# Expert weights laid out on the host in the order of the on-chip buffers: two transfers per pair of experts in place of four

## The reference

```python
def _L1_ffn_ref(hidden_states, router_weight, gate_up_proj, down_proj):
    # E = 64 experts, TOP_K = 8, CAPACITY = 256, H = 512, I = 192
    x = hidden_states.reshape(-1, H)
    probs = jax.nn.softmax(x @ router_weight.T, axis=-1)
    topw, topi = jax.lax.top_k(probs, K)
    topw = topw / jnp.sum(topw, axis=-1, keepdims=True)
    ...   # pos: each token's place in its expert's list; x_rep: x, K times over
    xe = jnp.zeros((E, C, H), x.dtype).at[flat_e, pos].set(x_rep, mode='drop')
    gu = jnp.einsum('ech,ehf->ecf', xe, gate_up_proj)
    g, u = jnp.split(gu, 2, axis=-1)
    ye = jnp.einsum('eci,eih->ech', jax.nn.silu(g) * u, down_proj)
    ...   # each token sums its K rows of ye, weighted by topw
```

## Time and profile before

| | |
|---|---|
| median of 3 runs | 5667.46 us (5666.89 to 5673.59) |
| the profiled execution: its own time | 5669.14 us |
| its span, first to last instruction | 5667.4 us |
| mean granted clock of PE | 0.919 |
| first layer of experts, SP's first weight load to POOL's last scatter | 2558.3 to 3324.0 us |
| second layer of experts, the same | 4880.0 to 5645.7 us |
| busy share of PE, DVE, ACT, POOL | 85%, 42%, 29%, 27% |
| q1's packets took, of 16 engines' span | 13.1% |
| q0's packets took | 12.3% |

### The profile page before, as it was taken

How to read it: one execution, slowest core, us unless ns; L and a number is a source line. 1 busy time by engine, 2 the same in 40 slices (tenths; PEclk the granted TensorE clock), 3 DMA queues, 4 the chain that set the end, 5 groups by cost and what they waited for, 6 DMA issues and landing times. The chain is left out here.

```text
span 5667.4 us, 66951 instructions
## 1 busy us (share of the span) xinstructions
PE 4820.4 (85%) x26288; PEld 2581.4 (46%) x26288; DVE 2362.7 (42%) x3233; ACT 1644.4 (29%) x2764; POOL 1527.4 (27%) x951
## 2 busy tenths in 40 slices
PE   6045988789999999985999949999999989589996
PEld 2013433333333333244655626666666654465654
DVE  1754588537666666744211122333333320512111
ACT  2511555120455555732111112222222210211111
POOL 0011000100577777011444430111111110044444
PEclk9567999899999999986999979999999999699998
DMA  1000000000000000013888840000000021368887
GB/s 46 0 9 17 16 0 0 0 32 1 1 1 1 1 1 1 1 55 112 221 224 226 226 87 25 29 23 29 31 29 31 21 101 61 131 172 224 218 225 164
DMA packets 223978, 395.83 MB, mean 70 GB/s; under 512 B 30480, under 2 KB 118544, under 8 KB 223632
## 3 DMA queue, kind: packets, MB, share of 16 engines
q1 hardware_dynamic: 166352, 249.13, 13.1%
q0 software_dynamic: 57344, 142.64, 12.3%
HBM read 288.88 MB, written 107.02 MB: 70 GB/s over the span
## 5 line engine op out<-in xcount | busy, mean ns | idle before, releaser
L2163 PE MATMUL linb_pr_ps<-lin_z,linb_wt 128*128 128x512 f32 x1536 | 677.8, 595 | 16.4 <-POOL linb_slope_own L2133 16.4
L1365 ACT ACTIVATE attc_prob<-attc_ps 128x512 f32<-128x512 f32 x1024 | 549.1, 596 | 443.0 <-PE attc_ps L1276 442.2
L1239 POOL TENSOR_TENSOR attc_acc<-attc_acc,attc_prob 128x2048 f32<-128x2048 f32 x120 | 547.9, 4566 | 121.6 <-ACT attc_prob L1365 109.2
L1389 DVE TENSOR_REDUCE attc_peak<-attc_ps 128x2 f32<-128x1024 f32 x384 | 469.6, 1225 | 258.0 <-PE attc_ps L1284 258.0
L1276 PE MATMUL attc_ps<-att_q,att_k 32*128 32x512 f32 x2048 | 528.6, 616 | 0.0
L1284 PE MATMUL attc_ps<-att_k,att_q 32*128 32x512 f32 x1536 | 450.0, 663 | 0.0
L2163 PEld LDWEIGHTS linb_pr_ps<-lin_z,linb_wt 128*128 128x128 f32 x1536 | 286.1, 191 | 342.1 <-issue 324.8
L2339 DVE SCALAR_TENSOR_TENSOR linb_gated<-linb_osb,linb_norm_w,linb_proj 128x512 f32<-128x512 f32 x64 | 94.4, 1474 | 668.1 <-ACT linb_osb L2266 668.1
L2140 POOL TENSOR_TENSOR linb_sq<-linb_osb 128x512 f32<-128x512 f32 x64 | 70.1, 1095 | 1039.0 <-ACT linb_osb L2266 1039.0
L1297 PE MATMUL attc_ps<-attc_prob,att_v 128*32 128x256 f32 (+1 forms) x3472 | 316.5, 437 | 0.3 <-ACT attc_prob L1365 0.3
L886 DVE TENSOR_TENSOR_SCAN ssmb_state<-ssmb_decay,ssmb_bu 128x2048 f32<-128x2048 f32 x64 | 279.7, 4409 | 78.9 <-ACT ssmb_decay L833 78.9
(11 more groups left out here) (510 smaller groups left out, 7652.8 us busy)
## 6 DMA issues: line engine op xcount, KB each, us to landing
moe1w_wgu<-in_L_ffn_gate_up_proj SPq DMA_DIRECT2D x32, 1536.0 KB
moe2w_wgu<-in_L_ffn_gate_up_proj SPq DMA_DIRECT2D x32, 1536.0 KB
moe1w_wd<-in_L_ffn_down_proj SPq DMA_DIRECT2D x32, 512.0 KB
gated_features<-linb_gated SPq DMA_DIRECT2D x64, 256.0 KB
moe2w_wd<-in_L_ffn_down_proj SPq DMA_DIRECT2D x32, 512.0 KB
linc_gt<-gated_features SPq DMA_DIRECT2D x7, 2048.0 KB
linb_wt<-in_L_attn_b_qkv_w SPq DMA_DIRECT2D x16, 768.0 KB
residual_rows<-residual SPq DMA_DIRECT2D x2, 4096.0 KB
```

The costliest lines, as they stand in the source:

```text
L1239: pool.tensor_tensor(acc[:, n % 2, :, :], before, prob[:, U % NP, :, :], ALU.add).then_inc(pool_done, 2 if at == 1 else 1)
L1365: nc.scalar.activation(prob[:, U % NP, h, :], ps[:, n % 3 if at < 0 else at % 6, :], ACT.Exp).then_inc(exp_done, 1)
L1389: V.tensor_reduce(peak[:, w // TT % 2, i % QH, 2 * hp:2 * hp + 2, b], ps[:, bank:bank + 2, :], axis=AX.X, op=ALU.max).then_inc(mx_used, 1)
L2163: last = nc.tensor.matmul(pr_ps[:, use % 2, :], wt[:, b, kind, k, :], z[:, k, t * NB:(t + 1) * NB], start=(k == 0), stop=(k == DT - 1))
```

## The change

The host reorders two inputs before the launch. `gate_up_proj` becomes (pair, partition, expert of the pair, k, column), so that what one partition of `wgu` takes is one stretch of 3072 numbers (12288 B) in DRAM; before, it was eight rows of 384 numbers (1536 B) in eight places. `down_proj` becomes (pair, partition, three rows of 512): the row of the first expert, that of the second, and the tail row, one stretch of 6144 B; before, it was three rows of 2048 B. `wd` and `wd_tail` become one buffer `wd` with three rows per partition, so each pair has two transfers in place of four. The bytes are the same, and PE reads the same numbers in the same order.

```diff
-        wd = W.sb("wd", [P, PW, 2, D])
-        wd_tail = W.sb("wd_tail", [P, PW, D])
+        wd = W.sb("wd", [P, PW, 3, D])
...
-        wgu_dram = g.dram["L1_ffn_gate_up_proj"].rearrange("e (k p) f -> p e k f", p=P)
-        wd_dram = g.dram["L1_ffn_down_proj"].rearrange("e p d -> p e d")
+        wgu_dram = g.dram["L1_ffn_gate_up_proj"]
+        wd_dram = g.dram["L1_ffn_down_proj"]
 
         def load_pair(sp, j):
             r = j % PW
-            sp.dma_start(wgu[:, r, :, :, :], wgu_dram[:, 2 * j:2 * j + 2, :, :]).then_inc(w_loaded[r], 16)
-            sp.dma_start(wd[:, r, :, :], wd_dram[0:P, 2 * j:2 * j + 2, :]).then_inc(w_loaded[r], 16)
-            for x in range(2):
-                sp.dma_start(wd_tail[x * TAIL:(x + 1) * TAIL, r, :], wd_dram[P:IN, 2 * j + x, :]).then_inc(w_loaded[r], 16)
+            sp.dma_start(wgu[:, r, :, :, :], wgu_dram[j, :, :, :, :]).then_inc(w_loaded[r], 16)
+            sp.dma_start(wd[:, r, :, :], wd_dram[j, :, :, :]).then_inc(w_loaded[r], 16)
...
-        W_LOADS = 4 * 16
+        W_LOADS = 2 * 16
...
-                        nc.tensor.matmul(ye_ps[:, y % 3, :], h[rows, j % 2, 2, cols], wd_tail[rows, j % PW, :],
+                        nc.tensor.matmul(ye_ps[:, y % 3, :], h[rows, j % 2, 2, cols], wd[rows, j % PW, 2, :],
...
+def expert_rows(a):
+    pairs = a.reshape(E_N // 2, 2, IN, D)
+    whole = pairs[:, :, 0:P, :].transpose(0, 2, 1, 3)
+    tails = pairs[:, :, P:IN, :].reshape(E_N // 2, P, 1, D)
+    import numpy as _np
+    return _np.concatenate([whole, tails], axis=2)
...
+    "L1_ffn_gate_up_proj": lambda a: a.reshape(E_N // 2, 2, DT, P, 2 * IN).transpose(0, 3, 1, 2, 4),
+    "L1_ffn_down_proj": lambda a: expert_rows(a),
```

More of the change, by code:

```diff
@@ L1490, in moe @@
             moe_routing(nc, g, name + "b", logits, index)
-        moe_experts(nc, g, name + "c", index, wgu, wd, wd_tail, w_loaded, load_pair, last)
+        moe_experts(nc, g, name + "c", index, wgu, wd, w_loaded, load_pair, last)
 def moe_logits(nc, g, name, logits, load_pair):
@@ L1802, in _, with moe_experts @@
                 lanes(q)
-def moe_experts(nc, g, name, index, wgu, wd, wd_tail, w_loaded, load_pair, last):
+def moe_experts(nc, g, name, index, wgu, wd, w_loaded, load_pair, last):
     with Layer(nc, name) as L:
```

## The result

| | before | after |
|---|---|---|
| device time, median of 4 runs | 5669.05 us (5666.89 to 5673.59) | 5716.23 us (5707.56 to 5728.7) |
| ratio to before | | 1.0088, 95% interval 1.0071 to 1.0105 |
| the profiled execution: its own time, its span | 5669.14, 5667.4 us | 5707.56, 5705.9 us |
| 28 rounds, first and second layer | 576.9, 577.5 us | 616.4, 618.4 us |
| DVE's wait at the two barriers | 12.6, 12.4 us | 0.8, 0.8 us |

The account below looks back on a forecast made before the run. It took the expert rounds to be bound by POOL's wait for scatters A to land, lengthened by weight loads. 5669.1 - 22 (barriers) + 62 (rounds) = 5709, less 1.7 to the median: 5707 us; range over all cases 5603 to 5772.

Parts of the forecast that it names:

- the two terms: Whole kernel: fewer starts at the two barriers give back 22 us; longer rows in 56 rounds cost 62 us.
- The barriers, -22 us: Barriers behind the router blocks: eight starts no longer held, saving 11.1 us in the first layer and 11.0 in the second.
- The rival that counts bytes: Router-block barriers: SP is held by bytes, so barriers stay and rounds grow, 5731 us; chance 0.07.
- The rounds, +1.1 us each, +62 us: Expert rounds: long rows ahead of scatters A lengthen each of 56 rounds, range +0.3 to +1.9 us.
- The price of the rows: Loads on q1: 472 ns per 12288 B row and 245 ns per 6144 B row, 5.74 us a load.
- all of it passes ahead of A, none is left for the gaps beside A: Rounds, q1: a load's 16 rows per engine fit within q0's 20 turns, so a round pays up to 5.74 us.
- the rival of equal bytes: Rounds: queues take turns of equal bytes, so each round is 0.7 us shorter, 5607 us; chance 0.30.
- A wait of 9.4 us in every round: POOL in the rounds: the wait between scatters A and B grows to near 9.4 us, a round to 21.7.
- Its test by the wait between A and B alone: POOL in the rounds: the forecast's sign is wrong if that wait is under 8.3 us.
- Whole rows: Loads on q1: long rows travel uncut, about 288 packets for a load in place of 1472.
- The rival of cut rows: Loads on q1: 12288 B stretches travel in pieces as short as now, rounds stay, 5647 to 5669 us; chance 0.05.
- At most 1.24 us a round to gain: Rounds: PE becomes the bound once its 1.24 us wait for gathered tiles is gone, 69 us in all.

Follow-up runs that it names:

- late_long: Changed kernel, long rows throughout, but SP starts a pair's load only after POOL has started scatters A four pairs earlier; 5744.28 us, ratio 1.0125.
- after_a_long: Changed kernel, all rows long, but SP starts a pair's load only when POOL has seen scatters A land; 5595.9 us, ratio 0.986.
- after_a_short: Against first_four (same rows): SP starts a pair's load only when POOL has seen scatters A land; 5571.57 us, ratio 0.9822 to the kernel before.
- the down-only kernels: Loads started just behind scatters A's start, only down weights loaded inside rounds (work left out); short rows 5559.5 us, long 5560.77, against the kernel before 0.9791 and 0.9794.
- first_four: Against the changed kernel: long rows only for pairs 0 to 3, short rows in four transfers for pairs 4 to 31; 5649.61 us, ratio 0.9956 to before.

## Why the prediction was right, and where it was not

The sign, the time (5707 against 5716) and the two terms came out. That the time is so close is in part luck: the two terms measure +57 us in place of the +40 of the forecast, and the medians show +47, with a router block whose clock differs between executions. Point by point:

- *The barriers, -22 us.* Measured -23.4. That what fills up is counted in rows is shown by the series: 88, 56 and 24 rows of equal bytes, DVE's wait 9 to 13, 5.6 to 5.7 and about 1 us. The rival that counts bytes is out.
- *The rounds, +1.1 us each, +62 us.* Measured +1.44, +80 us: within the +0.3 to +1.9 given, and mis-sized by taking the middle. The price of the rows was also low: by the DMA view of the first layer's rounds q1 took 28.8% of 616.4 us, 6.3 us a load and not 5.74. The full 5.74 us is what `late_long` pays, 10.05 and 10.27 behind A less the 4.43 of the earlier trace rows, 5.6 to 5.8, but as a late start and slower packets and not as a load ahead of A.
- *"all of it passes ahead of A, none is left for the gaps beside A".* This step failed. In the changed kernel 65 load packets still stood beside 64 of q0 late in A, and q1 was not empty before A's last packets. The prediction counted packets ahead of A, 20 turns against 16 rows, and took the turns to begin with the load. (Of the 36 packets per engine that it counted on q0, 5 to 6 carry 4 B each and 15 are of the gathers.) In fact 3 to 4 us of a load hold A back, with short rows and with long ones, and the rest runs beside A. Before, that rest was nearly free: of the 3.9 us paid, 5.43 - 2.33 = 3.1 are the late first packet and 4.80 - 4.39 = 0.4 the slower packets. With long rows beside it A takes turns with rows of 245 ns to 0.840 x 3.0 x 16 / 82 = 0.49 us: 10 of them lengthen A by 6.86 - 4.39 = 2.5 us, where 25 to 34 short ones cost 0.4 to 0.8. (The price of one long row is not constant: 0.25 us here, 0.28 in the changed kernel, but 0.11 for B of `after_a_long`.) That turns go by packet was right; so the rival of equal bytes is out: beside 0.40 MB of q1 it would have put as much of q0, and 0.13 was there. The rule cited from the Trainium skill (DMA: Bandwidth & Descriptors, section Queues, rings and completion order) agrees with the 65 to 64, where a turn of the load is one row.
- *A wait of 9.4 us in every round.* The mean was 8.63 and 8.97, most rounds 8 to 11 us, and about one in five 4 to 6. The prediction took every load to meet A and forgot that the next A waits for B. In one round of five the load meets B, whose landing then comes 9.2 to 12.2 us behind its start. In such a round A misses the load and waits little; the loss stands ahead of A. Its test by the wait between A and B alone, wrong in sign if under 8.3 us, can mislead, since only the sum of both idle times shows the loss: with tiles gathered four pairs ahead that wait was 7.8 us and the kernel still slower than before. That PE's wait for tiles grows (66.3 for 34.8 us) was foreseen; A does not wait for PE.
- *Whole rows.* The packets of the execution fell from 223,978 to 148,201, by 1184 for each of 64 loads: 1472 - 1184 = 288 each, as forecast. The rival of cut rows is out.
- *At most 1.24 us a round to gain.* Too low: in `after_a_short` the round gained 1.22 us and PE still waited 0.64 us for tiles, and the down-only kernels gained 1.4 to 1.7. PE's busy time was taken as fixed, but at a granted clock of 1.00 in place of 0.96 it fell from 542 to 525 us a layer.

## What to carry to other kernels

In this kernel long rows on one queue were cheap for themselves and dear for the short rows of a neighbour that something waits for, because the queues took turns by packet. So lengthen rows where a queue is filled ahead of a barrier, and test it with care beside scatters or gathers that something waits for. When a transfer lengthens another's wait, first move its start to where other work covers the wait: that gave 78 us with short rows here (`first_four` to `after_a_short`; 76 by the ratios) and 120 with long ones (the changed kernel to `after_a_long`; 129 by the ratios), while the rows' length decides 24 us between the two ends. Judge a wait in a loop together with the idle time ahead of it: a load that misses one pair of scatters may meet the next, and then the loss stands in another place.

## What the runs showed of the hardware beyond that

SP's start of a transfer at the router block took 0.3 to 0.7 us with 16 rows per engine and load, and at most 1.6 us with 24, 3.4 with 56 and 4.1 to 4.5 with 88 (the earlier trace rows and the kernels of the series). A scatter's first packets came 2.15 to 2.33 us behind its start with no load beside it. The granted clock of the same router block, in front of any changed instruction, was 0.50 from 2530 to 2550 us in one execution and 1.00 from 2540 to 2550 in another; over the whole block that was worth 10 to 14 us.
